# Graph layer with experts: matrices in a ring of three halves, two additions early

## What is computed

```python
xn = _layernorm(x)
# graph attention with a mask from 3072 typed edges
q, k, v = xn @ wq.T + bq, xn @ wk.T + bk, xn @ wv.T + bv
q2, k2, v2 = q @ wiq.T + biq, k @ wik.T + bik, v @ wiv.T + biv     # 16 heads of 64
attn = softmax(q2 k2^T / 8 + mask)
gnn = (attn @ v2) @ wo.T + bo
# a mixer on the same xn, with one position, then its layer norm
mix = layer_norm(xn + mixer(xn @ Wq, xn @ Wkv) @ Wo, ln_gamma, ln_beta)
x = x + gnn + mix
# experts: 8, two for each token, weights in bf16, and a shared one in float32
xf = _layernorm(x)
x = x + sum over the chosen experts of relu(xf*s @ up.T)**2 @ down.T
      + relu(xf @ shared_up.T)**2 @ shared_down.T
```

## Time and profile before

| | us |
|---|---|
| median of three runs | 359.8 (359.49 to 360.01) |
| the profiled execution | 359.56 |
| its span, first to last instruction | 358.2 |
| PE busy | 310.8 (87%) |
| DVE busy | 110.7 (31%) |
| ACT busy | 58.2 (16%) |
| POOL busy | 45.6 (13%) |

### The profile page before, as it was taken

One profiled execution on the slowest core, in us unless ns is written; L12 is line 12 of the kernel. 1 busy time (PEld: TensorE's weight loads), 2 busy tenths in 40 slices (PEclk: granted clock), 3 DMA queues, 4 the chain that ended last, 5 costly groups with the idle time before them and its releaser, 6 DMA issues.

```text
span 358.2 us, 2956 instructions
## 1 busy us (share of the span) xinstructions
PE 310.8 (87%) x1192; PEld 148.2 (41%) x1192; DVE 110.7 (31%) x242; ACT 58.2 (16%) x109; POOL 45.6 (13%) x84
## 2 busy tenths in 40 slices
PE   4999998999999999999879998899898864384667
PEld 4334334334343343533234565533454532142334
DVE  7608504501143439400822313200322330111111
ACT  1401000001003010300020033300323330120131
POOL 0611111111212111222300000000001030000000
PEclk9999999999999999999989999999999995866888
DMA  7999999999999999999999999999999999999996
GB/s 291 365 299 295 425 276 422 269 425 327 388 330 346 378 318 429 266 422 317 293 358 270 292 419 339 224 209 219 216 216 224 206 228 211 209 229 204 215 211 136
DMA packets 12425, 104.92 MB, mean 293 GB/s; under 512 B 1504, under 2 KB 1976, under 8 KB 3068
## 3 DMA queue, kind: packets, MB, share of 16 engines
q0 software_dynamic: 10944, 98.57, 95.5%
q1 hardware_dynamic: 1168, 6.01, 4.3%
q10 hardware_dynamic: 300, 0.16, 0.2%
HBM read 150.48 MB, written 0.39 MB: 421 GB/s over the span
## 4 chain that ended last, share of the span: by engine, by line
PE 64%; DMA 24%; DVE 4%; issue 4%; another core or an unknown queue 2%; ACT 2%; DVEq 0%
PE bank L832 30%; DMA stage<-in_expert_down 10%; PE bank L1010 10%; PE bank L990 8%; PE bank L968 6%; PE bank L1046 5%; DMA ring<-in_mat_wik 5%; DMA ring<-in_mat_wk 4%; DMA ring<-in_mat_mv 4%; PE bank L956 1%; PE bank L801 1%; ACT hbuf L440 1%; PE bank L816 1%; ACT xn L434 1%
## 5 line engine op out<-in xcount | busy, mean ns | idle before, releaser
L832 PE MATMUL bank<-ring,xnt 128*96 128x512 f32 x224 | 100.4, 606 | 1.1 <-ACT xnt L370 0.6
L832 PEld LDWEIGHTS bank<-ring,xnt 128*96 128x96 f32 x224 | 36.6, 166 | 59.7 <-issue 56.9
L1010 PE MATMUL bank<-stage,hbuf 128*96 128x512 bf16 (+3 forms) x198 | 46.2, 394 | 17.2 <-DMA stage<-in_expert_down 14.3
L990 PE MATMUL bank<-stage,late 128*96 128x512 bf16 (+1 forms) x192 | 44.7, 387 | 10.8 <-issue 10.3
L832 PE MATMUL bank<-ring,stage 128*96 128x512 f32 x96 | 42.1, 593 | 0.1
L1010 PEld LDWEIGHTS bank<-stage,hbuf 128*96 128x96 bf16 x198 | 24.4, 135 | 36.8 <-DMA stage<-in_expert_down 15.9
L990 PEld LDWEIGHTS bank<-stage,late 128*96 128x96 bf16 x192 | 24.2, 131 | 28.1 <-issue 16.4
L776 DVE TENSOR_TENSOR acc<-acc_t,acc 96x512 f32<-96x512 bf16 (+3 forms) x18 | 11.3, 628 | 58.9 <-ACT acc_t L459 58.7
L434 ACT ACTIVATE xn<-bank 96x512 bf16<-96x512 f32 (+2 forms) x26 | 14.5, 559 | 66.0 <-PE bank L990 59.8
L832 PEld LDWEIGHTS bank<-ring,stage 128*96 128x96 f32 x96 | 15.3, 163 | 23.2 <-issue 23.2
L763 DVE TENSOR_TENSOR xn<-xn 96x512 bf16<-96x512 bf16 (+1 forms) x24 | 9.6, 400 | 45.1 <-ACT xn L434 45.1
(11 more groups left out here) (161 smaller groups left out, 202.9 us busy)
## 6 DMA issues: line engine op xcount, KB each, us to landing
stage<-in_expert_up POOLq DMA_DIRECT2D x4, 2816.0 KB, 32.4
stage<-in_expert_down POOLq DMA_DIRECT2D x4, 2816.0 KB, 38.9
stage<-in_expert_down POOLq DMA_DIRECT2D x7, 1408.0 KB, 17.4
stage<-in_expert_up POOLq DMA_DIRECT2D x6, 1024.0 KB, 12.8
ring<-in_shared_down POOLq DMA_DIRECT2D x2, 2816.0 KB, 14.4
ring<-in_shared_up POOLq DMA_DIRECT2D x5, 1024.0 KB, 17.2
ring<-in_mat_wq SPq DMA_DIRECT2D x4, 1024.0 KB, 9.5
ring<-in_mat_wv POOLq DMA_DIRECT2D x4, 1024.0 KB, 11.7
```

Of the source, the lines that this page charges most:

```text
L832: ins = mm(bank[BANKS[m] + h][0:N, :], tiles(src)[:, k, :], w[:, kk, :], start=(k == 0), stop=(k == KT - 1))
L990: ins = mm(bank[4 + j][0:N, 0:c1 - c0], tiles(xe)[:, k, :], w[:, k, :], start=(k == 0), stop=(k == KT - 1))
L1010: ins = mm(bank[j][0:N, 0:c1 - c0], tiles(e_h)[:, t, :], w[:, t, :], start=(t == 0), stop=(t == TT - 1))
```

## The change

The ring has three slots of half a matrix (`PIECE` = 4096 floats a partition, rows of 16 KB, 2 MB) in place of five quarters. SP loads the first three halves. POOL loads a half when a whole half is used, on every second `used`; the shared up weights come in three pieces. TensorE waits once for each half (`half_landed`), and still signals after four k and after eight. `FIRST_AT` has new numbers. The ring is 1024 columns longer, and the buffer `late` is gone: the tokens' weights `w_all` lie behind the shared weights in the ring, the scaled tokens `xe` in the end of `hbuf`. The shift and the output bias lie in the stage buffer of expert 2, are spread at the start, and are added to x after the six `take_t`, before the edge codes. The scale lies in `hbuf` and is spread at `used` = 36. POOL's first expert load waits for the first half (2 MB) as it waited for the second quarter.

```diff
-PIECE = KT * HALF // 2
+PIECE = KT * HALF
 PIECES = 2
-SLOTS = 5
+SLOTS = 3
...
-FIRST_AT = [0, 1, 2, 7, 11, 17, 20, 22, 27, 33, 37, 39, 40, 43, 44]
+FIRST_AT = [0, 1, 4, 8, 12, 16, 20, 25, 29, 32, 38, 42, 44, 44, 44]
...
-        ring = sb("ring", [P, BUF], F32)
+        ring = sb("ring", [P, SLOTS * PIECE], F32)
...
-        gamma = ring[:, SLOTS * PIECE:SLOTS * PIECE + D]
...
-        late = sb("late", [P, EXPERTS * N + KT * N // 2], F32)
-        beta = late[:, 0:D]
-        w_all = late[:, 0:EXPERTS * N].rearrange("p (e n) -> p e n", e=EXPERTS)
-        xe = late[:, EXPERTS * N:EXPERTS * N + KT * N // 2].bitcast(BF16)
+        w_all = ring[:, BUF:BUF + EXPERTS * N].rearrange("p (e n) -> p e n", e=EXPERTS)
+        xe = hbuf[:, D - KT * N // 2:D].bitcast(BF16)
...
-        bias_o_b = hbuf[:, 0:D]
+        gamma = hbuf[:, 0:D]
+        beta = take(5376, D)
+        bias_o_b = take(6400, D)
...
-        def slot_of(piece):
-            return (piece + 1) % SLOTS
+        def slot_of(c):
+            return (c + 2) % SLOTS
...
+        def load_half(eng, c):
+            m, h = STEPS[c]
+            slot = slot_of(c)
+            landed = first_landed[c] if c < SLOTS else slot_landed[slot]
+            eng.dma_start(slots[slot], mats[m][h]).then_inc(landed, 16)
...
-            piece_landed(pool, 1)
+            half_landed(pool, 0)
             load(*FIRST_LOADS[0])
             pool.wait_ge(bias_v_landed, 16)
             nc.gpsimd.partition_broadcast(bias_v_b, bias_v_b[0:1, :]).then_inc(spread, 1)
-            pool.wait_ge(ln_landed, 32)
-            nc.gpsimd.partition_broadcast(gamma, gamma[0:1, :]).then_inc(spread, 1)
+            pool.wait_ge(ln_landed, 16)
             nc.gpsimd.partition_broadcast(beta, beta[0:1, :]).then_inc(spread, 1)
+            pool.wait_ge(bias_o_landed, 16)
+            nc.gpsimd.partition_broadcast(bias_o_b, bias_o_b[0:1, :]).then_inc(spread, 1)
             for used in range(1, len(STEPS) * PIECES + 1):
                 pieces_used(pool, used)
-                if used + SLOTS <= len(STEPS) * PIECES:
-                    load_piece(pool, used + SLOTS - 1)
-                else:
-                    load_shared_up(used + SLOTS - 1 - len(STEPS) * PIECES)
-                if used == len(STEPS) * PIECES:
-                    pool.wait_ge(pre_ready, 1)
-                    load_shared_up(SLOTS)
+                if used % PIECES == 0:
+                    c = used // PIECES - 1 + SLOTS
+                    if c < len(STEPS):
+                        load_half(pool, c)
+                    else:
+                        load_shared_up(c - len(STEPS))
                 if used == 36:
-                    pool.wait_ge(bias_o_landed, 16)
-                    nc.gpsimd.partition_broadcast(bias_o_b, bias_o_b[0:1, :]).then_inc(spread, 1)
+                    pool.wait_ge(ln_landed, 32)
+                    nc.gpsimd.partition_broadcast(gamma, gamma[0:1, :]).then_inc(spread, 1)
...
             for m, dst in (("wq", q1), ("wk", k1), ("wv", v1)):
                 for h in range(2):
                     take_t(m, h, dst)
 
+            dve.wait_ge(spread, 3)
+            link(tt(xs[0:N, 0:D], xs[0:N, 0:D], beta[0:N, :], ALU.add))
+            link(tt(xs[0:N, 0:D], xs[0:N, 0:D], bias_o_b[0:N, :], ALU.add))
+
             def codes(r):
...
             dve.wait_ge(spread, 4)
-            link(tt(xs[0:N, 0:D], xs[0:N, 0:D], beta[0:N, :], ALU.add))
-            link(tt(xs[0:N, 0:D], xs[0:N, 0:D], bias_o_b[0:N, :], ALU.add))
...
             def out_rows(m, h, src):
                 c = AT[m, h]
+                w = slots[slot_of(c)].rearrange("p (k n) -> p k n", n=HALF)
+                half_landed(pe, c)
                 for i in range(PIECES):
-                    piece = c * PIECES + i
-                    w = slots[slot_of(piece)].rearrange("p (k n) -> p k n", n=HALF)
-                    piece_landed(pe, piece)
```

More of the change, by code:

```diff
@@ L182, in gps_layer @@
         slot_landed = [sem(f"slot_landed{s}") for s in range(SLOTS)]
-        sh_up_landed = [sem(f"sh_up_landed{j}") for j in range(SLOTS + 1)]
+        sh_up_landed = [sem(f"sh_up_landed{j}") for j in range(SLOTS)]
         sh_dn_landed = [sem(f"sh_dn_landed{j}") for j in range(2)]
@@ L260, in program, with half_landed @@
             return lambda written: written(engine)
-        def slot_of(piece):
-            return (piece + 1) % SLOTS
-        def piece_landed(eng, piece):
-            if piece < SLOTS:
-                eng.wait_ge(first_landed[piece], 16)
-            else:
[L269 to L275, removed]
+        def slot_of(c):
+            return (c + 2) % SLOTS
+        def half_landed(eng, c):
+            if c < SLOTS:
+                eng.wait_ge(first_landed[c], 16)
+            else:
+                eng.wait_ge(slot_landed[slot_of(c)], 16 * (c // SLOTS))
+        def load_half(eng, c):
[3 more added lines that the diff above has]
+            eng.dma_start(slots[slot], mats[m][h]).then_inc(landed, 16)
         def pieces_used(eng, n):
@@ L286, in _ @@
             sp.dma_start(xs[0:N, 0:D], x).then_inc(x_landed, 16)
-            for piece in range(SLOTS):
-                load_piece(sp, piece)
+            for c in range(SLOTS):
+                load_half(sp, c)
             for j, (c0, c1) in enumerate(FINE[:-1]):
@@ L390, in _ @@
             act.wait_ge(shifted, 1)
-            act.dma_start(bias_o_b[0:1, :], bias_o).then_inc(bias_o_landed, 16)
+            act.dma_start(gamma[0:1, :], ln_gamma).then_inc(ln_landed, 16)
             nc.scalar.activation(scores[0:N, :], scores[0:N, :], ACT.Exp).then_inc(exps_ready, 1)
@@ L825, in out_rows @@
                 c = AT[m, h]
+                w = slots[slot_of(c)].rearrange("p (k n) -> p k n", n=HALF)
+                half_landed(pe, c)
                 for i in range(PIECES):
-                    piece = c * PIECES + i
-                    w = slots[slot_of(piece)].rearrange("p (k n) -> p k n", n=HALF)
-                    piece_landed(pe, piece)
-                    for kk in range(KT // PIECES):
-                        k = i * (KT // PIECES) + kk
-                        ins = mm(bank[BANKS[m] + h][0:N, :], tiles(src)[:, k, :], w[:, kk, :],
+                    for k in range(i * (KT // PIECES), (i + 1) * (KT // PIECES)):
+                        ins = mm(bank[BANKS[m] + h][0:N, :], tiles(src)[:, k, :], w[:, k, :],
                                  start=(k == 0), stop=(k == KT - 1))
@@ L964, in shared_up_part @@
                     if k == 0:
[L965 to L967 removed]
+                        pe.wait_ge(sh_up_landed[j], 16)
                     ins = mm(bank[4 + j][0:N, 0:c1 - c0], tiles(xnt[:])[:, k, :], w[:, k, :],
@@ L1061, in tiled @@
     def tiled(w):
-        return w.reshape(PIECES, KT // PIECES, P, 2, HALF).transpose(3, 0, 2, 1, 4)\
-            .reshape(4, P, PIECE)
+        return w.reshape(KT, P, 2, HALF).transpose(2, 1, 0, 3).reshape(2, P, PIECE)
     def by_columns(w, blocks):
```

2 lines of the change are left out of this document (1 added, 1 removed).

## The result

The changed kernel takes 362.8 us (median of 11 runs, 360.9 to 365.3), the kernel before 359.8 us in the same comparison (359.5 to 360.3): a ratio of 1.0081, 95% interval 1.0067 to 1.0095, or +3.1 us. The forecast was 362.8. The profiled execution took 362.83 us with a span of 361.5.

The account below looks back on a forecast made before the run. POOL's DMA queue was taken to set the end: its bytes' time plus every moment it is empty. Saving 1.1 us on loads and losing 4.1 in gaps gave +3.0 on 359.8, so 362.8 us, range 358.6 to 364.6.

Parts of the forecast that it names:

- Fewer and longer loads: Matrices and shared up weights: 25 DMAs in place of 50, same bytes, saving 1.1 us.
- the two equations: Two never-empty queue stretches: 31a + 38.75b = 94.79 and 6a + 33b = 79.75; a 0.045 us per DMA, b 2.41 per MB.
- the rows of 22 KB: Shared down weights' loads: 2.41 us per MB, taken to show 16 KB rows cost no more per byte than 8 KB.
- The stall: Edge codes: two early DVE additions delay TensorE's four code products by 2.47 us; their wait grows from 1.21 to 3.7 us.
- The clock: Behind the edge-code stall: TensorE's granted clock falls from 2.4 to 1.2 GHz for a while, losing 1.6 us.
- rival 1: Edge-code stall: the clock holds at 1.00, delay and gaps are 2.5 us, time 361.2 us; chance 0.2.
- Lead and need: POOL's queue: lead 4.0 us at wo's second half, 4.7 at mv's first; need 3.8; TensorE's 4.1 us delay opens gaps.
- The place of the gaps: DMA share under 1 for one to two us near 79, 121 and 160 us; gaps 4.1 us in all.
- rival 3: Ring loads: TensorE waits for whole halves to land, its delay grows by 1 to 2 us, 364.9 us; chance 0.1.
- Rival 2: POOL's queue never runs dry: 358.7 us if the delay is 2.5, 359.9 if 4.1; chance 0.25.
- Rival 4: Ring loads: rows of 16 KB give nothing, 363.9 us; no chance of its own given.
- The sum: Whole kernel: -1.1 us from the loads and +4.1 from gaps give +3.0, so 362.8 us against the 359.8 median.

Follow-up runs that it names:

- The last two kernels: Changed kernel with both additions behind the mask steps, halves stored as two blocks with 8 KB rows: one DMA per half 361.79 us, one per block 361.3 us.
- the profiled run with one load earlier: Changed kernel with expert 2's first load at the 37th quarter in place of the 38th, ahead of wo's second half: 361.95 us, ratio 1.0067.
- the kernel with the empty queue: Kernel before, with the first half of the shared down weights issued only with the second: 362.2 us, ratio 1.0063.
- the kernel with the additions moved: Changed kernel with the shift and output bias additions behind the mask steps, ahead of the bias additions of wiq: 358.62 us, ratio 0.997.
- the other table: Changed kernel with both additions behind the mask steps and FIRST_AT putting expert loads earlier among the halves: 364.4 us, ratio 1.0133.
- the kernel with one addition early: Changed kernel with the output bias addition behind the mask steps and the shift still ahead of the edge codes: 359.64 us, ratio 1.0002.
- old table: Changed kernel with both additions behind the mask steps and the kernel before's FIRST_AT over halves: 360.61 us, ratio 1.0029.

## Why the prediction was right, step by step

**Fewer and longer loads.** Expected -1.1 us; without the stall the kernel is 359.74 - 358.62 = 1.1 us faster. The sum put it to the number of DMAs, at 0.045 us each (the two equations give 0.048). The last two kernels and the packets show that the rows carry it: the matrices have 2,816 rows fewer, at 7 ns each on 16 engines. The number was right, its carrier was not: in the kernel before, DMAs and rows rise together, and the rows of 22 KB that were to bound the cost of a row could not do it, since 7 ns in a row of 836 ns are under 1%.

**The stall.** 1.21 to 3.72 us, as expected. TensorE starts the codes 2.3 us later than before (62.15 for 59.86), 0.2 less than the sum.

**The clock.** In the profiled run it fell right behind the stall, and cost 1.7 us of TensorE's work (1.6 expected). In the profiled run with one load earlier, which has the same stall, it is 0.50 in the whole of 62.4 to 66.0 us, and that run took 363.2. Of the 11 runs of the changed kernel two at a mean clock of 0.952 and 0.953 took 360.9 and 361.0 us, six at 0.948 had a median of 362.6, three at 0.943 and 0.944 took 363.1 to 365.3. That fits a clock that held in two of them (rival 1 says 361.2), but it does not show it. The mean over the span does not tell a fall behind the stall from one elsewhere: the kernel with the empty queue has a mean of 0.948 in its profiled run and a clock of 1.00 from 20 to 180 us. The medians of two kernels make the fall dearer (2.7 us); falls that last longer, as in the run at 363.2, would do that, and how often they come is open.

**Lead and need.** The lead came out at 4.4 us at wo and 4.8 at mv (4.0 and 4.7 expected). The need of 3.8 us was taken from POOL's first load. As a restart time it was mis-sized: an empty queue costs 3.0 (9.6 - 6.6). As what the whole loses it held roughly: with 3.8, a delay of 4.0 in the kernel before, with its least lead of 5.8, gives 2.0 us (measured 361.72 - 359.74 = 2.0); the delay of 2.3 without a fall gives 2.3 + 3.8 - 4.4 = 1.7 (measured 1.55); the changed kernel 4.0 + 3.8 - 4.4 = 3.4 us over the kernel with the additions moved, against 4.2 measured (362.83 - 358.62). With 3.0 all three come out 0.6 us or more too low.

The landings of the changed kernel say where the rest goes. A half lost 0.2 us at wiv, where the load ahead of it had 2.8 us to go at its issue, but 1.7 at mk with 3.6 to go, 1.0 at mv with 3.2, and 1.1 at wo with 3.9: needs of 3.0, 5.3, 4.2 and 5.0 us, around the 3.8. At the same places the 16 engines drift apart: the first and the last finish a load 0.9 us apart behind wiv, 2.2 at mk, 2.8 at wo. Why a single engine falls behind by about a us is open. A queue that runs low is not the only occasion: in the kernel with the additions moved the distance grows from 1.7 to 3.0 us at 191 us, in a load that was issued when the one ahead of it still had 7.7 us to go.

**The place of the gaps.** Expected near 79, 121 and 160 us, 4.1 us in all. By the packets the mean engine falls behind the kernel with the additions moved by 0.9 us at 80 to 86, 0.9 at 110 to 124, 0.8 at 125 to 130 and hardly (0.2) at 160. But a load has landed only when the last of its 16 engines is done:

| load | issued + to landing, changed kernel | the same, additions moved | later by |
|---|---|---|---|
| wiv, first half | 78.56 + 8.0 = 86.6 | 74.48 + 11.9 = 86.4 | 0.2 |
| mk, first half | 107.36 + 10.2 = 117.6 | 103.87 + 11.7 = 115.6 | 2.0 |
| mv, first half | 122.80 + 9.1 = 131.9 | 119.31 + 9.7 = 129.0 | 2.9 |
| wo, second half | 160.76 + 10.0 = 170.8 | 157.41 + 9.3 = 166.7 | 4.1 |

Counted so, the gap at wiv cost next to nothing, there was one more at mk, those at mv and wo came as forecast, and up to wo they add up to 4.1 us. The last up weights, issued when the last quarter of the ring is used, come at 181.37 us, 3.5 us later than before (177.87); 4 to 5 were expected.

**Rivals.** TensorE waits for no half in the changed kernel, so rival 3 did not happen. Its mechanism is real, as the other table shows (5.8 us); that it stayed away is owed to FIRST_AT. Rival 2, no dry queue, would have been right with a fully held clock and a need under 2 us. Rival 4, nothing gained by rows of 16 KB, is refuted by the 1.1 us and by the 7 ns of a row.

**The sum.** -1.1 and +4.1 were expected, -1.1 and +4.2 measured. The mechanism is the one forecast, but the agreement to a tenth is in part luck. The need of 3.8 us came from a single start beside a busy queue; with the measured restart of 3.0 and the measured lead of 4.4 the same sum gives 4.0 + 3.0 - 4.4 = 2.6, so 361.3 us in place of 362.8. And the median stands among runs from 360.9 to 365.3.

## What to carry to other kernels

Where TensorE and the DMA queue are both full, TensorE's own delay, the clock's fall behind it and the restart of the queue add up, less the queue's lead: an edit of 2.5 us on an idle engine cost 4.2 us. Put work that nothing waits for behind the point at which a full engine waits for yours, and read the engines' order, not their busy shares, to find it. More lead by earlier loads is no free cure: bytes put ahead of what the full engine needs next make that engine wait, and the same clock falls.

## What the runs showed that I had not expected

- The clock fell behind shorter waits than the two of 3.4 and 3.6 us that the prediction relied on: 1.71 us before 30.15 (0.60 behind it) and 2.22 before 101.03 (0.72). Yet 2.47 us before 61.00 left it at 1.00 in the profiled run, and 2.10 before 76.52 was not followed by a fall either. The idle time just before is a poor guide in that range. The Trainium skill (TensorE: Matmul & The Clock Gate, "What's actually happening") calls the slow stretch at the start of one kernel variable from run to run. No kernel here has two profiles, so whether a fall in mid-kernel varies like that is not shown.
- The mean clock that comes with each run goes with its time only roughly: runs of the kernel with one addition early at 0.948 took 359.6 us and at 0.953 360.9. It holds every fall of the span. The spread of a kernel is 4 us (changed kernel) to 5 us (old table), where the kernel before has 0.8 to 1.2.
- Feeding TensorE with 16 matmuls that compute nothing won 2.7 us by the medians.
- A row of a load costs 7 ns beyond its bytes, a DMA nothing that shows.
- An issue on an empty queue costs 3.0 us beyond the bytes' own time, in landings; the page's DMA row in tenths shows none of the gaps that cost 3 to 4 us here. The landings of successive loads, less their own time, do.
